# Attention sums of a graph network by lanes of 416 edges, with a running maximum per batch of 16, in place of one-hot products behind a pass for the largest logit

## The reference, cut to what matters

```python
h = maximum(layernorm(x), 0)
hc = (h[:, :240] @ Wc.T).reshape(n, 4, 64)         # the message of a node
s, d = ...                                          # per head, from hc and the last 16 features
e = leaky_relu(s[src] + d[dst], 0.2)                # one logit per edge and head
m = segment_max(e, dst);  ee = exp(e - m[dst])
a = ee / segment_sum(ee, dst)[dst]
x = x + segment_sum(hc[src] * a[..., None], dst).reshape(n, 256) + h
```

## Time and profile before

| what | value |
|---|---|
| median of 3 runs | 3491.63 us (3487.08 to 3497.18) |
| the profiled execution, time | 3510.2 us |
| its span | 3508.4 us |
| granted TensorE clock over the span, share of full speed | 0.79 |
| busy PE / DVE / ACT / POOL | 2221.9 / 1850.7 / 1199.1 / 1362.5 us |
| DMA | 426.14 MB, mean 121 GB/s |
| instructions | 52320 |

### The profile page before, as it was taken

One profiled execution on the slowest core, in us unless ns is written; L12 is line 12 of the kernel. 1 busy time (PEld: TensorE's weight loads), 2 busy tenths in 40 slices (PEclk: granted clock), 3 DMA queues, 4 the chain that ended last, 5 costly groups with the idle time before them and its releaser, 6 DMA issues. The chain is left out here.

```text
span 3508.4 us, 52320 instructions
## 1 busy us (share of the span) xinstructions
PE 2221.9 (63%) x13309; PEld 1727.8 (49%) x13309; DVE 1850.7 (53%) x3986; ACT 1199.1 (34%) x3751; POOL 1362.5 (39%) x1373
## 2 busy tenths in 40 slices
PE   2567776767799968997999826666666621111104
PEld 1456665666699934555444426666666410000003
DVE  3245555557799944203899725454445623333342
ACT  1111111113577711112233236666566232222221
POOL 1266666664000032001000055555554256666663
PEclk9878888889899989998999867777777655555556
DMA  2466666660566500001333244444443045555553
GB/s 60 149 179 189 192 189 184 189 198 18 148 152 151 135 0 19 0 0 41 126 135 135 73 96 107 107 103 108 104 104 91 23 136 165 186 184 180 185 195 121
DMA packets 352045, 426.14 MB, mean 121 GB/s; under 512 B 173988, under 2 KB 249880, under 8 KB 351973
## 3 DMA queue, kind: packets, MB, share of 16 engines
q1 hardware_dynamic: 288435, 251.32, 24.0%
q0 software_dynamic: 63280, 173.75, 17.8%
q10 hardware_dynamic: 258, 0.21, 0.0%
HBM read 353.01 MB, written 71.66 MB: 121 GB/s over the span
## 5 line engine op out<-in xcount | busy, mean ns | idle before, releaser
L627 POOL DMA_INDIRECT msg_rows<-message_source_table,msg_index x416 | 401.4, 965 | 309.2 <-issue 183.4
L627 POOL DMA_INDIRECT att_rows<-att_table,att_index x416 | 397.3, 955 | 282.1 <-remote 117.8
L1905 POOL DMA_INDIRECT best_rows<-message_source_table,lane_source x416 | 407.5, 980 | 232.4 <-issue 126.4
L723 ACT ACTIVATE att_rows<-att_rows,att_exps 128x64 f32<-128x64 f32 x1664 | 409.0, 333 | 8.8 <-issue 8.4
L2013 DVE SCALAR_TENSOR_TENSOR best_state<-best_state,lane_line,best_rows 128x256 f32<-128x256 f32 x416 | 201.9, 485 | 383.1 <-issue 241.7
L755 PE MATMUL msg_ps_sum<-msg_by_edge,msg_rows 128*128 128x128 f32 x1664 | 260.5, 320 | 168.8 <-DVE aggT L687 100.3
L1962 PE MATMUL best_ps_self<-w_selfT,hT 128*125 128x256 f32 x100 | 51.7, 671 | 480.7 <-DVE x L2023 281.8
L755 PEld LDWEIGHTS msg_ps_sum<-msg_by_edge,msg_rows 128*128 128x128 f32 x1664 | 245.7, 231 | 195.6 <-issue 178.5
L755 PE MATMUL att_ps_sum<-att_by_edge,att_rows 128*128 128x128 f32 x1664 | 321.7, 325 | 12.1 <-issue 11.7
L1927 ACT ACTIVATE best_rows<-best_rows,lane_weight 128x256 f32<-128x256 f32 x416 | 177.2, 496 | 436.0 <-DMA best_rows<-message_source_table,lane_source 426.2
L687 DVE TENSOR_TENSOR aggT<-aggT,att_ps_sum 128x384 f32 x416 | 227.4, 547 | 177.0 <-remote 110.9
(11 more groups left out here) (280 smaller groups left out, 4106.3 us busy)
## 6 DMA issues: line engine op xcount, KB each, us to landing
msg_window<-message_window_table SPq DMA_DIRECT2D x416, 128.0 KB
best_states<-best_state SPq DMA_DIRECT2D x104, 512.0 KB
attr_rows<-in_edge_attr SPq DMA_DIRECT2D x103, 192.0 KB, 3.4
msg_line<-place_line SPq DMA_DIRECT2D x52, 256.0 KB
attr_line<-mask_line SPq DMA_DIRECT2D x52, 256.0 KB
attr_carry<-carry_line SPq DMA_DIRECT2D x52, 256.0 KB
logit_within<-within_line SPq DMA_DIRECT2D x52, 256.0 KB
logit_blocks<-block_line SPq DMA_DIRECT2D x52, 256.0 KB
```

Of the source, the lines that this page charges most:

```text
L627: nc.gpsimd.indirect_dma_start(rows[:, s, t, :], None, table, bass.IndirectOffsetOnAxis(ap=index[:, s, t:t + 1], axis=0)).then_inc(self.ro ...
L723: last = nc.scalar.activation(head, head, ACT.Copy, scale=exps[:, s % BUFS, t, h:h + 1])
L1905: nc.gpsimd.indirect_dma_start(rows[:, g % SLOTS, t, :], None, table, bass.IndirectOffsetOnAxis(ap=self.lane_source[:, g * TG + t:g * TG + ...
```

## The change

The attention layer becomes two blocks, `attention_tables` and `attention_pass`; `logit_pass`, `logit_table`, `attention_update` and the attention branch's use of `sum_pass` go.

- The table row has 268 floats: per head 64 values and a constant 1.0 (so that the sum of the weighed ones is the denominator), 4 source terms, 4 destination terms. POOL writes the ones (L1458), adds h to x in one instruction (L1459), and scatters the destination terms of each tile to `att_terms` in HBM, at the first edge of each node (L1463, 25 indirect DMAs; the array is cleared by one transfer first). `first_edge` comes from `mlp`, where SP stores and loads the counts of the search.
- `attention_pass` works by lanes. A scan spreads the destination terms over each lane's edges. POOL issues one gather of the lane's first node and 416 gathers (L1639) as straight code, into 48 row buffers, and waits once per 16 for the batch 48 edges back. Per batch of 16 edges DVE forms the logits, scans forward for the running maximum (L1727), scans backward to give all edges of one node in the batch the same maximum (L1730), and subtracts; ACT takes one `exp` of 128x68; DVE scales the carried sum (L1775), weighs four edges per instruction (L1742), and adds each edge to the state (L1749), times 0 where a node begins. SP writes the states, four edges to a transfer. The batches are 25 of 16, then 8, 4 and 4 edges.
- Behind the last edge come the join over lanes, now with weights for the differing maxima, 25 gathers by `last_edge`, division and addition to x in fifths.
- `prepare` loses the two lines; one piece of its work that sits in the message tables runs four tiles earlier; `lane_source` is loaded in the attention tables rather than in `pool_table`.

```diff
+BATCH = 16
+CHUNK_BUFS = 3
+BATCHES = [(t, BATCH) for t in range(0, LANE - BATCH, BATCH)] + [(LANE - BATCH, 8), (LANE - 8, 4), (LANE - 4, 4)]
...
-            lines = ((self.mask_line, mask), (self.place_line, rel16), (self.block_line, block16),
-                     (self.within_line, within16), (self.carry_line, carry))
+            lines = ((self.mask_line, mask), (self.place_line, rel16), (self.carry_line, carry))
...
-                    nc.gpsimd.memset(self.aggT[:], 0.0)
+                    for h in range(H):
+                        nc.gpsimd.memset(out[:, :, h * HS + HD:(h + 1) * HS], 1.0).then_inc(ones_set, 1)
+                    nc.gpsimd.tensor_tensor(self.x[:], self.x[:], self.h[:], ALU.add)
+                    pool.wait_ge(cleared_out, 16)
+                    for b in range(NB):
+                        pool.wait_ge(termed, b + 1)
+                        nc.gpsimd.indirect_dma_start(
+                            self.term_line, bass.IndirectOffsetOnAxis(ap=self.first_edge[:, b:b + 1], axis=0),
+                            out[:, b, AS:AR], None).then_inc(spread, 16)
+                    pool.wait_ge(spread, 16 * NB)
...
+                    for k, (t0, n) in enumerate(BATCHES):
+                        if t0 >= ring and t0 % BATCH == 0:
+                            pool.wait_ge(moved, moves_upto(t0 - ring + BATCH - 1))
+                        for t in range(t0, t0 + n):
+                            nc.gpsimd.indirect_dma_start(
+                                rows[:, t % ring, :], None, self.attention_table,
+                                bass.IndirectOffsetOnAxis(ap=self.lane_source[:, t:t + 1], axis=0)
+                            ).then_inc(rows_in[k % SLOTS], 16)
...
+                    def weigh(k, j):
...
+                        nc.vector.tensor_tensor(
+                            of, of, of_batch(exps, k)[:, :, at:at + TG].rearrange("p h t -> p t h").unsqueeze(3)
+                            .to_broadcast([P, TG, H, HS]), ALU.mult).then_inc(moved, 1)
...
+                    def step(t, starts):
...
+                        dve.wait_ge(moved, moves_upto(t) - 1)
+                        nc.vector.scalar_tensor_tensor(
+                            out=state[:, t % held, 0:H * HS],
+                            in0=carried[:] if starts else state[:, (t - 1) % held, 0:H * HS],
+                            scalar=self.lane_carry[:, t:t + 1], in1=rows[:, t % ring, 0:H * HS], op0=ALU.mult,
+                            op1=ALU.add).then_inc(moved, 1)
...
-            k.attention_tables()
-            k.logit_pass(largestT)
-            k.logit_table(largestT)
-            k.sum_pass("att", k.attention_table, D + H, k.logit_rows, 2 * H, attention=True)
-            k.attention_update()
+            k.attention_tables(layer)
+            k.attention_pass()
```

More of the change, by code:

```diff
@@ new lines, in _ @@
+                    pool.wait_ge(fix_out, 16)
+                    for b in range(NB):
+                        nc.gpsimd.indirect_dma_start(neigh[:, b, :], None, states, bass.IndirectOffsetOnAxis(
+                            ap=self.last_edge[:, b:b + 1], axis=0)).then_inc(rows_in[b // fifth], 16)
+                @block.scalar
+                def _(act):
+                    for k, (t0, n) in enumerate(BATCHES):
+                        act.wait_ge(terms, 6 * (k + 1))
+                        nc.scalar.activation(flat(exps, k), flat(logit, k), ACT.Exp).then_inc(exps_made, 1)
+                    act.wait_ge(shut, 4)
+                    nc.scalar.activation(share[:], share[:], ACT.Exp).then_inc(shares, 1)
+                    act.wait_ge(spread, 1)
+                    nc.scalar.copy(shares_all[:], ps_share[:]).then_inc(spread_kept, 1)
+                    act.wait_ge(shut, 8)
+                    nc.scalar.activation(before[:, 0:2, :], before[:, 0:2, :], ACT.Exp).then_inc(shares, 1)
@@ new lines, in _ @@
+                    dve.wait_ge(cleared, 5)
+                    nc.vector.tensor_scalar(open_line[:], open_line[:], FLT, None, ALU.mult).then_inc(cleared, 1)
+                    dve.wait_ge(lists_in, 16)
+                    dve.wait_ge(node_in, 16)
+                    for h in range(H):
+                        nc.vector.tensor_tensor_scan(term[:, h, :], self.lane_carry[:], line[:, :, h],
+                                                     node[:, AS + h:AS + h + 1], ALU.mult, ALU.add).then_inc(filled, 1)
@@ new lines, in _ @@
+                    dve.wait_ge(back, 2)
+                    nc.vector.tensor_tensor(heads(whole[:, 0:H * HS]), ps_sums[:],
+                                            before[:, 1, :].unsqueeze(2).to_broadcast([P, H, HS]), ALU.mult
+                                            ).then_inc(fixed, 1)
+                    dve.wait_ge(fixed, 2)
+                    nc.vector.tensor_tensor(whole[:, 0:H * HS], whole[:, 0:H * HS], first[:, 0:H * HS], ALU.add
+                                            ).then_inc(fixed, 2)
@@ L1792, in pool_table @@
+        self.before.update((s.name, 16) for s in self.fix_events)
+        for j, s in enumerate(rows_in):
+            self.before[s.name] += 16 * tiles_upto(final - (final - j) % SLOTS) + (16 * fifth if j < 5 else 0)
+        for j in range(2):
+            self.before[states_out[j].name] += 16 * len(range(j * BATCH, LANE, 2 * BATCH)) * BATCH // TG
     def pool_table(self):
```

569 lines of the change are left out of this document (281 added, 288 removed).

## The result

| | before | changed |
|---|---|---|
| median | 3489.36 us (3486.86 to 3497.18, 4 runs) | 3052.11 us (3051.34 to 3060.27, 4 runs) |
| profiled execution, span | 3510.2, 3508.4 us | 3051.8, 3050.0 us |
| instructions | 52320 | 30724 |

What follows compares the result with a forecast made beforehand. POOL's queue of gathers was to bound the new attention pass. Terms 57.5 + 584.7 + 9 + 51 = 702.2 against 1163.0, with 2.5 from `prepare` 463.3 less: 3510.2 to 3046.9, less 18.6 for the median, 3028 us; range 2960 to 3140.

Steps and rivals of the forecast that it cites:

- the ring: Attention pass, the 48 row buffers: POOL's wait for the batch 48 edges back was to be hidden, 41 us against 67.
- tables: Attention tables: 57.5 us instead of 69, first fold held by POOL's addition, 25 scatters at 1.24 us outlasting PE.
- entry and 416 gathers: Attention pass: block entry 1.0, node gather 1.25 and 416 gathers at 1.40 us, together 584.7 us.
- after the last gather: End of the attention pass: landing, last logits and `exp`, carried sum, weighing, steps and leftover batch work, 9 us.
- repair to norm3: Behind the last edge: join over lanes, 25 gathers by last edge at 1.24 us, division; 51 us, update before 38.
- Pace: Attention pass: one gather every 1.40 us, 416 of them 582.4 us; each 0.1 us per edge is 42 us.
- the disturbed row: Earlier lane pass timeline: gathers beside DVE's steps at 1.07 + 0.30 = 1.37 us, taken as upper bound for one gather.
- Rival B: Attention pass: gathers wait out two-SBUF-input DVE instructions; by chance pace 1.46, +25, 3053 us; whole instruction 3153; chance 0.10.
- DVE hidden: Attention pass: DVE's work of 16.5 us per batch of 16 edges stays below POOL's 22.4 us.
- A: Attention pass: gathers undisturbed by DVE, 1.24 us throughout, 67 us less, 2962 us; chance 0.11.
- C: Attention pass: DVE's queue is slow, 0.70 us per queued instruction +0 to +20 us, at 1.40 +416, 3444; chance 0.15.
- D: Attention pass: POOL and DVE take turns, 51 us per batch, 3.2 us per edge, +749, 3777 us; chance 0.02.

Runs made afterwards that it cites:

- experiment 1: Changed kernel with the exponentials of a batch written to PSUM instead of SBUF; 2804.92 us, ratio 0.8953 to the kernel before on the same chip.
- experiment 11: Changed kernel with exponentials in PSUM and the lane maximum pass as straight code, on a slower-kind chip; 3083.58 us, ratio 0.8782 to the kernel before.
- experiment 2: Changed kernel with each weighing of four edges split into four one-edge instructions, both inputs still in SBUF; 2810.29 us, ratio 0.8963 to the kernel before.

## Why the prediction was right, point by point

The forecast was 3028 us, measured 3052, within the range. The signs named for it came: gathers of 1.11 us with 0.30 between them, no wait for the ring, DVE at 15 of 22.6 us and waiting at L1715. Two missed: the tables took 65 us and not under 60, and the way to norm3 56 and not about 50. Against the profiled execution the sum was 463.3 us, measured 458.4. Its own terms:

| term | forecast | measured |
|---|---|---|
| tables | 57.5 | 65.3 |
| entry and 416 gathers | 584.7 | 589.9 |
| after the last gather | 9 | 13.7 |
| repair to norm3 | 51 | 56.0 |
| logit pass and table | 0 | 0 |
| stores in `prepare` | -2.5 | -1.5 |

- **Pace.** 1.40 was picked a little above the 1.37 of the disturbed row, with the long instructions in mind; 1.415 was measured. The mechanism behind the number was only half right: the earlier trace rows showed a little for each gather beside short steps; here it is not a little for every gather, but 0.76 or 0.94 us for three gathers in sixteen and nearly nothing for the others. Rival B put the remainder at 0.22 us per gather, on average; measured (68/416) 0.16. The hold is full for the rest of the instruction, as B said. By B's own terms the weighings should cost 4 x 1.24²/2/22.4 = 0.14 us per gather and the steps 16 x 0.485²/2/22.4 = 0.08; measured were 0.15 (62/416) and under 0.02. So the weighings are met as often as chance has it, and the steps' remainders hardly at all. B's mechanism was the right one, and the forecast chose against it by one disturbed gather of 1.07 us, called an upper bound, while the gathers here reach 1.9. That a picked 1.40 came within 0.015 is in part luck. B's time, 3053, stands nearest to the measured 3052, but that is luck too: its pace is 19 us too long for the pass, and the other terms' misses make up for it.
- **Tables.** Two terms failed. Scatters were priced as gathers, 1.24 us apart, and stood 1.48 apart (1.18 each), 25 x 0.24 = 6 us; landing and block change were 4.5 us instead of 3; the first scatter came 1 us late. The held fold (12.5 us) came as forecast, and the first product at 20.6 us into the tables against 21.0.
- **Last batches and repair.** The small batches' logit chains of eight instructions stand one behind the other, 4.7 us more than the term. Behind the last step the spread of the factors over PE and ACT and two scans took 2275.91 - 2264.07 = 11.8 us to the first gather by last edge, as summed, but these 25 gathers were held by the divisions too: 1110 ns instead of 950, so 25 x 0.16 = 4 of the 5 us.
- **Untouched stages.** The layer's miss of 22.7 us was hidden by the rest: the stages outside the layer were together some 19 us shorter than in the profiled execution of before (message pass 7, lane maximum pass 5, the rest in small parts). So it is luck that the sum of 463.3 lies only 5 from 458.4. As 18.6 was just what the prediction took off to come to the median, its 3028 against 3052 is the layer's miss and 1 us of `prepare`.
- **DVE hidden.** Estimated 16.5 us per batch, measured about 15. POOL's wait for the ring never came.
- **Rivals.** A (1.24) was wrong for the kernel as it is, and it is what experiment 1 nearly reaches on the faster kind, 0.98 + 0.30. C did not occur in the changed kernel's attention pass, but in experiment 11, where the gathers ran free on the slower kind. D did not occur: DVE and POOL overlap but for the holds.
- **What was not seen.** The 708 us of the old sum pass were taken as its price; 156 of them belong to that chip. The prediction read the stages' hand-overs as the cause; the same code runs in 552.

## What to carry to other kernels

Where POOL issues gathers back to back, a DVE instruction beside them that reads two SBUF tiles for long is to be looked at first: on the faster kind, putting the small operand in PSUM freed 51 us of the pass, and splitting the instruction into quarters 36 (578.6 against 614.7 from the first gather to the first by last edge). On the slower kind it cost 20 us instead (experiment 11), because DVE fell behind. Before a looped or long pass is replaced, see whether its idle time is its own: the same kernel on another chip shows it, and here a third of the gain was that chip's. Leaving work out (the logit pass and its table, 348 us) was the part of this change that paid on both kinds.

## What the runs showed of the hardware that was not expected

- A single POOL scatter among 25 back-to-back DVE additions with two SBUF inputs took 8.50 us, its neighbours 1.18: here the hold lasted over a chain of instructions. In experiment 2 it did not, 24 gathers got in behind the first of four; what decides stays open. The Trainium skill (SBUF — State Buffer, Who interferes with whom) has the shared ports as an exclusive lock that blocks the second fully. The result's trace agrees with it for a DVE instruction with two SBUF inputs (1.7 to 1.9 us for a gather), and experiment 1 for one with an input from PSUM (0.95).
- POOL's addition of h to x held a DVE instruction on 128x8 elements that reads SBUF (L1482, 12.52 us), but not the clearing of `lane_source` just before it, which only writes: 0.41 us in the middle of the addition.
- Two kinds of chips: 3490 to 3510 and 3130 to 3135 us for the same kernel, at the same times for the PE-bound logit pass and for single DVE and POOL instructions. The time goes where DVE works beside POOL's unbroken gathers: in experiment 11 the steps then stood 0.7, 1.4, 2.1 or further multiples of 0.7 us apart. On the faster kind no two steps of the lane maximum pass stood 1.4 us apart. Straight code does not remove it, in either pass (experiment 11). What differs between the chips stays open; no run told it apart.
